# A decoder block's experts spread over the whole loop period, with the gate computed in halves

## The reference

```
x = x + agent_attention(layernorm(x))            # 16 heads of 64, 8 pooled queries ("agents") per head:
                                                 #   p1 = softmax(agent k^T); p2 = softmax(q agent^T); out = p2 (p1 v)
x = x + cross_attention(layernorm(x), ctx)       # 16 heads of 8, causal mask, keys and values from ctx
x = x + experts(layernorm(x))                    # 16 experts of 64 + 2 shared

gate: scores = softmax(x gate_w^T); + gate_b; 4 groups of 4 experts, the 2 groups with the
      largest sum of their two best are kept; of these the 2 best experts get their softmax weight
experts: y = sum_e weight_e * (silu(x We1 + be1) * (x We3 + be3)) We2 + be2;  z = the same with the shared ones
```

## Time and profile before

| | us |
|---|---|
| median of 3 runs | 1292.38 (1291.53 to 1292.47) |
| the profiled execution | 1290.0 |
| its span, first to last instruction | 1288.3 |
| TensorE busy | 1069.6 (83%), mean granted clock 0.878 |
| VectorE busy | 646.9 (50%) |
| ScalarE busy | 456.3 (35%) |
| GpSimd busy | 116.5 (9%) |

### The profile page before, as it was taken

One profiled execution on the slowest core, in us unless ns is written; L12 is line 12 of the kernel. 1 busy time (PEld: TensorE's weight loads), 2 busy tenths in 40 slices (PEclk: granted clock), 3 DMA queues, 4 the chain that ended last, 5 costly groups with the idle time before them and its releaser, 6 DMA issues.

```text
span 1288.3 us, 26430 instructions
## 1 busy us (share of the span) xinstructions
PE 1069.6 (83%) x11562; PEld 892.9 (69%) x11629; DVE 646.9 (50%) x1633; ACT 456.3 (35%) x790; POOL 116.5 (9%) x117
## 2 busy tenths in 40 slices
PE   6657879988798969988799887989699887998687
PEld 5644767787676858677676876768586776767565
DVE  2535276624657166542757246571665427561353
ACT  4432453234422353234432344223432345322221
POOL 7100010002000020001000020000200010000100
PEclk9788889978899889988899788998899888995589
DMA  6100010001000010000100010000100000000000
GB/s 164 34 1 2 2 34 1 10 10 34 1 9 10 2 34 1 10 10 2 34 9 2 10 34 1 9 10 2 33 1 10 10 2 1 9 10 2 1 1 17
DMA packets 28404, 18.50 MB, mean 14 GB/s; under 512 B 7393, under 2 KB 26882, under 8 KB 28290
## 3 DMA queue, kind: packets, MB, share of 16 engines
q1 hardware_dynamic: 26402, 12.35, 3.6%
q0 software_dynamic: 1280, 4.20, 1.1%
q10 hardware_dynamic: 608, 0.27, 0.1%
HBM read 12.62 MB, written 4.19 MB: 13 GB/s over the span
## 4 chain that ended last, share of the span: by engine, by line
PE 65%; DVE 20%; ACT 7%; POOL 4%; issue 3%; DVEq 0%; another core or an unknown queue 0%; POOLq 0%; ACTq 0%
PE banks L508 8%; PE banks L651 6%; PE banks L634 5%; PE banks L497 4%; PE banks L498 4%; PE banks L499 4%; PE banks L695 3%; DVE xn L1086 3%; PE banks L539 3%; PE banks L467 3%; ACT PXUT L943 3%; PE banks L626 3%; DVE sil L1172 2%; PE banks L604 2%; PE banks L775 2%
## 5 line engine op out<-in xcount | busy, mean ns | idle before, releaser
L887 ACT ACTIVATE sil<-banks,b 128x512 f32<-128x512 f32 x144 | 99.5, 691 | 247.2 <-PE banks L499 244.5
L508 PE MATMUL banks<-w,hT 128*128 128x128 f32 x1152 | 156.7, 280 | 29.1 <-DVE xn L1185 18.0
L1172 DVE SCALAR_TENSOR_TENSOR sil<-banks,b,sil 128x512 f32<-128x512 f32 x128 | 95.8, 748 | 167.1 <-ACT sil L887 154.9
L508 PEld LDWEIGHTS banks<-w,hT 128*128 128x128 f32 x1152 | 153.5, 196 | 31.6 <-DVE xn L1185 18.5
L1240 DVE RECIPROCAL rx<-banks 128x32 f32<-128x32 f32 x32 | 11.4, 358 | 243.1 <-PE banks L651 243.1
L943 ACT ACTIVATE PXUT<-banks 128x512 f32<-128x512 f32 x128 | 69.4, 609 | 154.8 <-PE banks L634 154.8
L1179 DVE TENSOR_TENSOR hT<-sil,banks 128x512 f32<-128x512 f32 x128 | 88.0, 687 | 15.1 <-remote 11.0
L1223 DVE TENSOR_REDUCE mx<-banks 128x8 f32<-128x512 f32 x128 | 79.5, 684 | 26.5 <-PE banks L604 26.5
L467 PE MATMUL banks<-ident,xn 128*128 128x128 f32 x192 | 38.2, 365 | 56.5 <-DVE xn L1086 56.5
L497 PE MATMUL banks<-xnT3l,w1h 128*128 128x512 f32 x144 | 77.7, 540 | 7.6 <-ACT sil L887 6.4
L695 PE MATMUL banks<-pooled,A 128*128 128x128 f32 x512 | 73.6, 303 | 12.2 <-ACT M L880 10.3
(11 more groups left out here) (203 smaller groups left out, 1858.3 us busy)
## 6 DMA issues: line engine op xcount, KB each, us to landing
xin<-in_x SPq DMA_DIRECT2D x8, 512.0 KB, 4.5
cin<-in_ctx SPq DMA_DIRECT2D x8, 512.0 KB, 5.8
out_x<-xn POOLq DMA_DIRECT2D x16, 256.0 KB, 2.8
KQ<-in_L_attn_Wqkv SPq DMA_DIRECT2D x3, 512.0 KB, 5.2
KQ<-in_L_ffn_We SPq DMA_DIRECT2D x2, 512.0 KB, 4.3
KQ<-in_L_attn_Wo SPq DMA_DIRECT2D x1, 512.0 KB, 7.9
w<-in_L_ffn_We SPq DMA_DIRECT2D x1, 512.0 KB
KQ<-in_L_ffn_ws SPq DMA_DIRECT2D x2, 64.0 KB, 4.4
```

What stands on the lines that cost most here:

```text
L508: mm(ps(name)[:, P * t:P * t + P], hT[:, k % 2, P * t:P * t + P], w2[:, pair[k], :], start=(n == 0 and t == 0), stop=False, skip_group_che ...
L887: nc.scalar.activation(sil[:, k % 2, :], ps(f"H1_{k}")[:], ACT.Silu, bias=b1[:, pair[k]:pair[k] + 1]).then_inc(sil_ready, 1)
L1172: V.scalar_tensor_tensor(sil[:, k % 2, :], ps(f"H3_{k}")[:], b3[:, p:p + 1], sil[:, k % 2, :], ALU.add, ALU.mult).then_inc(hid_ready, 1)
```

## The change

- The attention keeps its ring of four banks for everything, also in the second pass (`attention_tiles` lists all tiles in order, over all periods); H1, H3, C and Y keep their own banks all the time. So units can stand anywhere: 0 at the start of the period, 13 between the steps 1 and 2 of the first pass, 14 to 17 in the second pass.
- The gate, the normalisation of the experts' tokens and the transpositions for them are done in halves of four tiles. Half 0 of group `g` is normalised and gated at the end of its own period; half 1 in the next.
- In the second pass ScalarE does silu 14, the exps of steps 0 and 1, silu 15, silu 16, the exps of steps 2 and 3, silu 17. On TensorE unit 15 and unit 17 stand between `scores_T` and `values`; unit 14 and unit 16 ahead of `scores_T`.
- The next group is normalised (`apply_a(xin, ...)`) between the maxima of steps 1 and 2, its transpositions stand behind step 3. The keys are made behind unit 9 instead of unit 0.
- There are two residual buffers `xr` in turn, changed in place; `xe` and `xo` go.

```diff
+        add(g, *[f"V_{k}" for k in range(4)])
+        add(e, "xnT3_1")
+        add(g, "s1_0", "s1_1", "s2_0")
+        add(e, "combS_0", "gate_1")
...
+        for u in range(UX):
+            add(g, *[f"ST_{XQ * u + q}" for q in range(XQ)])
+            if u:
+                add(g, f"OT_{u - 1}")
+            add(g, f"O_{u}")
...
+            add(n, f"M_{2 * u}", f"M_{2 * u + 1}")
+            if u:
+                add(g, f"Yx_{u - 1}")
...
-            "f": banks[4:6], "o": banks[6:7], "yx": banks[7:8]}
# GpSimd
+            def rstd_e(g, c):
+                pool.wait_ge(var3_ready, 2 * g + c + 1)
+                ts = slice(QT * c, QT * c + QT)
+                nc.gpsimd.tensor_tensor(rstdb[:, ts], vb[:, ts], mhalf[:, ts], ALU.pow).then_inc(rstd3_ready, 1)
# TensorE, both(e, g)
+                unit(e, 0)
                 if g is not None:
                     pe.wait_ge(ctxT_ready, 2 * g + 2)
                     for n in range(4):
                         values_of(g, n)
                 if e is not None:
-                    four(e, "xnT3_0", xn3, 0)
-                    four(e, "xnT3_1", xn3, 1)
+                    turn_3(e, 1)
                 if g is not None:
                     scores_1(g, 0)
                     scores_1(g, 1)
                     scores_2(g, 0)
                 if e is not None:
+                    turn_weights(e, 0)
+                unit(e, 1)
+                if e is not None:
+                    gate_scores(e, 1)
...
+                unit(e, 9)
                 if g is not None:
                     keys_of(g, 0)
                     keys_of(g, 1)
+                unit(e, 10)
                 if g is not None:
                     pe.wait_ge(xn_ready, 2 * g + 2)
                     four(g, "xnT2_0", xn, 0)
...
+                    scores(g, 0)
+                    scores(g, 1)
+                unit(e, 13)
+                if g is not None:
+                    scores(g, 2)
+                    scores(g, 3)
+                    if nxt is not None:
+                        front_ctx(nxt)
+                        front_xn(nxt)
+                    turn_shifts(g)
...
+                    if u % 2 == 0:
+                        unit(e, 14 + u)
                     if g is not None:
+                        scores_T(g, u)
+                    if u % 2:
+                        unit(e, 14 + u)
+                    if g is not None:
+                        if u:
+                            turn_O(g, u - 1)
+                        values(g, u)
# ScalarE, both(e, g)
                 if e is not None:
                     for n in range(2):
                         moved(e, f"combT_{n}", ...
+                if g is not None:
+                    K_moved(g, 0)
+                    K_moved(g, 1)
                 silu(e, 10)
...
+                    if u % 2 == 0:
+                        silu(e, 14 + u)
+                    if g is not None:
+                        for q in range(XQ):
+                            exp_x(g, XQ * u + q)
+                    if u % 2:
+                        silu(e, 14 + u)
# VectorE, both(e, g)
-                    apply("e", xe, xn3, rstd3_ready, e + 1, xn3_ready)
+                    hidden(e, 0)
+                    gate_best(e, 0, 1)
+                    gate_weights(e, 0)
+                    apply_e(e, 1)
                 if g is not None:
                     soften(g, 0)
...
                 if e is not None:
-                    gate(e)
+                    gate_groups(e, 1)
                 if g is not None:
                     normalise_2(g, 0)
...
+                    maxima(g, 0)
+                    maxima(g, 1)
+                hidden(e, 13)
+                if nxt is not None:
+                    apply_a(xin, 2 * nxt + 1)
+                if g is not None:
+                    maxima(g, 2)
+                    maxima(g, 3)
+                    split_shifts(g)
...
+                result(e, 1)
+                if g is not None:
+                    gate_shift(g, 0)
+                    add_x(g, UX - 1)
+                    norm_e(g, 1)
+                    gate_groups(g, 0)
+                    gate_best(g, 0, 0)
```

More of the change, by code:

```diff
@@ L421, in both @@
                     store(e, 0)
-                if g is not None and g + 1 < GROUPS:
-                    rstd_a(2 * g + 3)
+                if g is not None:
+                    if g + 1 < GROUPS:
+                        rstd_a(2 * g + 3)
+                    rstd_e(g, 0)
+                    low(g, 0)
                 if e is not None:
@@ L712, in front_M, with turn_3, gate_scores @@
                     moments(g, n)
+            def turn_3(g, c):
+                pe.wait_ge(xn3_ready, 2 * g + c + 1)
+                four(g, f"xnT3_{c}", xn3, c)
+            def gate_scores(g, c):
+                name = f"gate_{c}"
+                wait_free(pe, g, name)
+                pe.wait_ge(xnT3_ready, 2 * g + c + 1)
+                for t in range(QT):
+                    t0 = P * (QT * c + t)
+                    last = mm(ps(g, name)[:, E * t:E * t + E], xnT3[:, t0:t0 + P], gwT[:], start=True, stop=True)
+                last.then_inc(fulled(g, name), 1)
@@ L714, in both, with queries @@
+            def queries(g):
+                for c in range(2):
+                    name = f"QT_{c}"
+                    wait_free(pe, g, name)
+                    pe.wait_ge(xnT_ready, 4 * g + 3 + c)
+                    mm(ps(g, name)[:], xwT[:, 0, :], xnT[:, 512 * c:512 * c + 512], start=True,
+                       stop=True).then_inc(fulled(g, name), 1)
             def both(e, g):
@@ L797, in both @@
-                for k in range(7, 11):
-                    unit(e, k)
+                unit(e, 10)
                 if g is not None:
@@ L803, in both @@
                 unit(e, 11)
-                if g is not None:
-                    for c in range(2):
-                        wait_free(pe, g, f"QT_{c}")
-                        pe.wait_ge(xnT_ready, 4 * g + 3 + c)
-                        mm(ps(f"QT_{c}")[:], xwT[:, 0, :], xnT[:, 512 * c:512 * c + 512], start=True,
-                           stop=True).then_inc(fulled(f"QT_{c}"), 1)
-                unit(e, 12)
                 if e is None:
@@ L841, in both @@
+                    if g is not None and u:
                         project(g, u - 1)
-                    values(g, u)
-                turn_O(g, UX - 1)
-                project(g, UX - 1)
+                if g is not None:
+                    gate_scores(g, 0)
+                    turn_O(g, UX - 1)
+                    project(g, UX - 1)
             run(pe, both)
@@ new lines, in norm_a, with norm_e @@
+            def norm_a(src):
+                for t in range(T):
+                    last = V.bn_stats(stats["a"][:, t, :], src[:, t, :])
+                link(last)
+                moments_of("a", var_ready, 0, T)
+            def norm_e(g, c):
+                dve.wait_ge(xattn_added, UX * g + 2 * c + 2)
+                for t in (QT * c + 2, QT * c + 3):
+                    last = V.bn_stats(stats["e"][:, t, :], xr[g % 2][:, t, :])
+                link(last)
+                moments_of("e", var3_ready, QT * c, QT * c + QT)
@@ L1142, in gate @@
-                link_e(V.tensor_tensor(tv[:], oh[:, 0], oh[:, 1], ALU.add))
-                cw = comb[:, :, 0:E]
-                part = [combs[:, :, E * k:E * k + E] for k in range(3)]
-                V.tensor_tensor(cw, tv[:], orig[:], ALU.mult)
-                link_e(V.tensor_tensor(part[0], tv[:], orig[:], ALU.mult))
-                V.tensor_tensor(ga[:], cw, part[0], ALU.subtract)
-                link_e(V.tensor_tensor(part[1], cw, part[0], ALU.subtract))
-                V.tensor_tensor(part[2], ga[:], part[1], ALU.subtract).then_inc(comb_ready, 1)
+                link(last)
@@ L1316, in both @@
-                for k in range(9, 11):
-                    hidden(e, k)
-                result(e, 0)
+                    hidden(e, 10)
                 hidden(e, 11)
-                hidden(e, 12)
-                for u in range(UX):
-                    if g is not None:
-                        maxima(g, u)
-                    hidden(e, 13 + u)
-                if g is not None:
-                    split_shifts(g)
-                hidden(e, 17)
-                result(e, 1)
-                if g is None:
-                    return
```

715 lines of the change are left out of this document (369 added, 346 removed).

## The result

The changed kernel takes 1338.7 us (median of four runs, 1336.5 to 1342.7) against 1291.95 for the kernel before beside it: a ratio of 1.0372, 95% interval 1.034 to 1.0405. It is slower, as forecast, but by 47 us where 24 were forecast.

What follows compares the result with a forecast made beforehand. TensorE's waits and clock bound it. Six usual periods at +8.7 waits and -3.5 clock (+31 us), first +10, seventh -8, last -9: +24 on 1290.0, 2.4 more for the median: 1316 us; forecast's own range 1298 to 1350, stated range 1255 to 1365.

Steps and rivals of the forecast that it cites:

- wait 1: Turn of the period: TensorE waits for half 1's tokens (`xnT3_1`) behind VectorE's gate work, about 7.3 us a period.
- wait 2: Agents' probabilities: unit 3 waits 1.5 us behind silu 2, the second transposition 3.3; together 4.8 us a period.
- wait 3: Keys: TensorE waits for the queries' tokens while ScalarE scales the keys ahead of silu 10, 4.6 us a period.
- wait 4: Maxima: step 3 waits 4.6 us for step 2's banks, the next group's transpositions 1.6; together 6.2 us a period.
- wait 5: Exponentials: values of steps 0 and 2 wait 2.2 + 1.9 us; last unit's result and last projection add 0.7 and 0.6.
- +8.7: TensorE's waits in a usual period: 28.3 us and 1.1 for small ones against 20.7 before, so 8.7 us more.
- The old waits: Waits for gate's weights, normalised tokens, an expert's silu and first output half go: 16.1 of 20.7 us a period.
- the clock term: Usual period: three or four clock drops lose 10.5 us against 14 before, so -3.5; bounds 3 and 20.
- First, seventh and last period: Periods outside the six alike: first +10 us (8 without clock), seventh -8, last -9 with half the gate done before.
- Table loads and GpSimd: ScalarE's loads go from 16 to 60 at 1.28 us, six of eight a period in waiting time; GpSimd's halves gain nothing.
- A: Faster rival: spread units hold the clock, loss 3 instead of 14 us a period, 1269 us; chance 0.27.
- B: Much slower rival: every wait drops the clock, 20 us lost a period, 1381 us; over 1350 given 0.14.

Runs made afterwards that it cites:

- experiment 2: Changed kernel with the keys' matmuls ahead of unit 8 and their scaling ahead of silu 9: 1327.3 us, ratio 1.0269.
- experiment 5: Changed kernel with VectorE doing the gate's groups of half 1 ahead of hidden 2 instead of behind it: 1326.8 us, ratio 1.0281.
- experiment 1: Changed kernel with the tokens of half 1 scaled earlier on VectorE, between the gate's groups and its first choice: 1338.5 us, ratio 1.0356.
- experiment 7: Changed kernel with 6 and 4 extra matmuls of 512 columns ahead of the values of steps 0 and 2, second pass: 1325.7 us, ratio 1.0287.
- Experiment 6: Changed kernel with the next group's moments between scores and values in steps 0 and 2 of the second pass: 1307.6 us, ratio 1.0126.
- five edits: Changed kernel with half 1's tokens, keys, next group's normalisation and gate's groups early, and moments ahead of values in steps 0 and 2: 1236.8 us, ratio 0.9593.
- experiment 3: Changed kernel with the next group normalised ahead of and behind hidden 11 instead of between maxima 1 and 2: 1350.75 us, ratio 1.0463.
- experiment 4: Changed kernel with 26 extra matmuls of 512 columns while TensorE waits for half 1's tokens at the turn: 1336.1 us, ratio 1.0351.
- experiment 9: The kernel with five edits, without the earlier normalisation of the next group: 1248.6 us, ratio 0.9677.
- four edits: Changed kernel with half 1's tokens, keys, next group's normalisation and gate's groups all early: 1276.4 us, ratio 0.9901.

## Why the prediction was right, and where it fell short

**Waits: right, nearly one by one.** Per period forecast and read: wait 1 7.3 and 7.35; wait 2 4.8 and 1.47 + 3.33 = 4.80; wait 3 4.6 and 4.63; wait 4 6.2 and about 5.2; wait 5 5.4 and 5.35 (2.23 and, for step 2, 0.67 + 1.12; 0.80 and 0.55 at the end). Idle time rose by 7.7 us a period, (947.74 - 774.71 - 896.42 + 769.38)/6, against +8.7. The old waits went as said. That experiments 2 and 5 took just these waits out shows their causes; experiment 1 shows that wait 1 belongs to VectorE's whole chain and not to the tokens' place in it.

**The step that failed is the clock term, "10.5 against 14: -3.5".** A period's clock loss went from 13.2 to 12.3 us (half of 26.5 and of 24.5 us busy at the low level), so -1.0, and the mean granted clock of the six periods is 0.91 (0.90 before) where I had put 0.92 to 0.94. I expected three or four drops; the period from 481.6 us has six. Two begin at waits 1 and 3; the other four begin in or behind scores and values, less than 2 us behind shorter waits (1.4 us in pieces, 2.4 in pieces, 2.23, and 0.67 + 1.12). I had expected the units of 512 columns in the second pass to end each drop sooner. They did shorten the drop of the earlier trace rows; but it lasted 17 us only in the period that I had read, 13.7 in one other and 10.2 in four, so less was to be had than I took. The change also moves the next group's moments from ahead of a step's values to behind them, and I had priced that order only as wait 5: what the moments lose to half clock went from 9.5 to 27 us over the kernel, while the values' loss fell from 16 to 9. The moments' group of rows of the kernel before (that of the changed kernel stands in experiment 7):

```profile
L695 PE MATMUL banks<-pooled,A 128*128 128x128 f32 x512 | 73.6, 303 | 12.2 <-ACT M L880 10.3 <-DVE pooled L1263 1.9
```

Experiment 6 puts them back in two steps, and 7 shows the clock's part.

**A cost I had not seen: +1.8 us a period of "work"** (115.0 to 116.8). Sixteen mask matmuls of a score step took 0.64 us before, four banks side by side. Where they now wait for banks that VectorE frees 0.6 us apart, two or three of them start alone, 0.6 us apart, and the rest behind them (a lone row's 0.40 us is a modelled length, the starts are exact). A step before, then step 1 after:

```profile
683.22 0.64 PE L596 MATMUL banks<-maskb,pick 32*64 32x512 bf16 x16
```

```profile
564.39 0.40 PE L620 MATMUL banks<-maskb,pick 32*64 32x512 bf16 x1 [0.83 <-DVE mx L1331]
```

Their busy time rose from 25.3 to 48.1 us over the kernel, 8 of these 23 us by clock. In a usual period it is 2.1 us more work, other work 0.3 less. It lies in wait 4, which so costs 7.3 us instead of 6.2.

Together: 7.7 + 1.8 - 1.0, some 8.55 instead of 5.2, six times 3.35 = 20 of the 22.7 us that were missing. First, seventh and last period: +11.5 - 14.2 = -2.7 against -7 forecast, another 4; against that, the runs' median is 0.05 above the profiled execution where I had added 2.4. That these periods came near their forecasts is in part luck. The first was to be 8 us longer by waits and 2 by clock; its idle time stayed (26.8 before, 26.3 after), since as much waiting went elsewhere as came behind exponentials, and its clock loss rose from 8.5 to 17.1 us. In the seventh and last, where 8 us were to go with the normalisation and the half clock and 9 with half of the gate, idle time rose by 4 and the clock loss fell by 19: the whole gain there is clock.

**Table loads and GpSimd: right.** 60 loads, none dearer than 1.28 us; the waits for silu 2 are 10.5 us in 8, as put into wait 2.

**The rivals.** A (the clock is held, 1269) is refuted for this order, but its mechanism exists: with five edits the clock loss is 77.5 us over the kernel. B (every wait drops the clock, 20 us lost a period) fails by its size: 12.3 are lost. What B and A share, that a wait has a drop of its own, is what experiments 3, 4 and 9 speak against: taking a wait out or filling it moved drops elsewhere. That waits play no part is not shown: each of the six drops in the period from 481.6 us begins in a wait or less than 2 us behind one.

**Open.** Whether the short wait ahead of them or the sparse scores and values themselves bring the level down, no run separates. Why the level falls in one pass at the values and in the next behind them, with the same instructions at the same distances, I could not settle either; usual periods of one execution differ by 3 us by this (157.1 and 160.3 in the changed kernel, clock loss 10.3 and 16.3), and so do runs of the kernel with four edits (1267 to 1286).

## What to carry to other kernels

Split a span into idle time, work and clock loss before and after an edit, and see first that both traces hold the same instructions: here work stayed within 1% in all variants, so that each edit's result could be read as waits taken out and clock paid back. A wait that one busy engine causes moves to that engine's next customer when its queue is only reordered; take out waits whose engine has idle time of its own (the keys, the gate's groups), and judge edits together, because alone one cost 12 us and in company it gained 11. Try dense matmuls ahead of sparse ones, where TensorE waits for the sparse ones' operands: it paid in the second pass (experiments 6 and 7), not at the turn (4).

## What the runs showed that I had not expected

- While the values keep TensorE busy without a gap the granted clock still falls to 0.5 in them, 1.5 us behind a wait of 2.23 us (593 to 596 us above); six or four dense matmuls of 512 columns in the wait ahead of the values took most of that away (moments 349 to 301 ns a piece, against 303 before the change).
- Taking out idle time can make a kernel slower: 7 us less idle, 21 more clock loss, ratio 1.0463 against 1.0372.
- Sixteen mask matmuls on four row groups took 0.64 us where their four banks were free; where VectorE freed the banks one by one, they started 0.6 us apart.
